# Second edge stage of a graph network kernel: own rows weighted on ScalarE, a quad ahead, in four copies instead of one VectorE operation

## The reference

```python
def gcn_conv(x, W, b, src, dst, n_nodes):
    xw = x @ W
    deg = segment_sum(ones, dst, n_nodes)
    dis = where(deg > 0, rsqrt(maximum(deg, 1e-12)), 0.0)
    norm = dis[src] * dis[dst]
    msgs = norm[:, None] * xw[src]
    return segment_sum(msgs, dst, n_nodes) + b
...
h = maximum(_layernorm(x), 0.0)
x = x + gcn(h)              # src, dst with a self-loop for every node
h = maximum(_layernorm(x), 0.0)
```

## Time and profile before

| | |
|---|---|
| time, median of 3 runs | 6671.95 us (6667.89 to 6674.51) |
| profiled execution: its own time | 6683.69 us |
| its span, first to last instruction | 6681.9 us |
| granted TensorE clock, mean | 0.848 of full |
| busy: PE, PEld | 4418.0 us (66%), 3717.4 us (56%) |
| busy: DVE, ACT, POOL | 3833.9 us (57%), 2944.6 us (44%), 3487.0 us (52%) |
| operation `OWN<-OWN,dis` on DVE, stages C1 and C2 | 98 times, median 693 ns |

### The profile page before, as it was taken

The page is one execution under the profiler, slowest core; times in us unless marked ns, Lnnn a source line. Parts: engine busy times, 40 slices in busy tenths (PEclk is TensorE's granted clock), DMA queues, the critical chain, the costliest instruction groups (busy, mean ns, idle before and its releaser), DMA issues. The chain is left out here.

```text
span 6681.9 us, 125449 instructions
## 1 busy us (share of the span) xinstructions
PE 4418.0 (66%) x28875; PEld 3717.4 (56%) x28950; DVE 3833.9 (57%) x13851; ACT 2944.6 (44%) x7261; POOL 3487.0 (52%) x4337
## 2 busy tenths in 40 slices
PE   4888888888788668877798966630660480282065
PEld 3666666666566666667787856630550370272065
DVE  5777777777544883347677767730650460261186
ACT  3777777777432333335576755530230130031043
POOL 3444444444470747327575665027457556556666
PEclk9999999999999659998999987765895795696576
DMA  3555555555442665448543444222232232232143
GB/s 98 184 187 187 187 187 186 186 186 186 128 115 70 198 181 136 115 122 218 151 118 96 113 113 116 82 69 53 73 95 53 61 103 58 51 102 70 43 115 91
DMA packets 1002707, 815.71 MB, mean 122 GB/s; under 512 B 103820, under 2 KB 836818, under 8 KB 1002616
## 3 DMA queue, kind: packets, MB, share of 16 engines
q1 hardware_dynamic: 908536, 650.27, 31.5%
q0 software_dynamic: 94080, 164.48, 10.3%
HBM read 359.28 MB, written 459.01 MB: 122 GB/s over the span
## 5 line engine op out<-in xcount | busy, mean ns | idle before, releaser
L839 POOL DMA_INDIRECT G<-table,idx_all x1568 | 1522.7, 971 | 1308.3 <-issue 670.6
L1411 PE MATMUL PS<-G,S 128*128 (+2 forms) x4312 | 852.3, 304 | 6.4 <-DMA G<-table,idx_all 2.4
L1411 PEld LDWEIGHTS PS<-G,S 128*128 128x128 f32 x4312 | 731.4, 220 | 55.8 <-issue 48.2
L839 POOL DMA_INDIRECT G<-table,idx_l x588 | 581.6, 989 | 336.2 <-issue 178.7
L1734 ACT ACTIVATE CR<-PS 65x128 f32<-65x128 f32 (+3 forms) x1078 | 289.1, 268 | 1021.2 <-PE PS L1411 1009.6
L1411 PE MATMUL PS<-CR,LO 97*128 97x128 f32 (+1 forms) x4312 | 655.3, 301 | 64.4 <-ACT CR L1734 64.4
L1408 PE MATMUL PS<-ident,ES 128*98 128x128 f32 x16 | 4.2, 420 | 1002.3 <-DVE ES L470 1002.3
L1411 PE MATMUL PS<-G,FS 128*65 (+2 forms) x3234 | 521.2, 301 | 216.9 <-DVE den L1343 100.7
L1411 PEld LDWEIGHTS PS<-CR,LO 97*128 97x128 f32 x4312 | 606.9, 217 | 75.7 <-ACT CR L1734 75.7
L792 POOL DMA_INDIRECT XIN<-in_x,idx_x x196 | 187.5, 957 | 846.0 <-ACT GN L1734 732.4
L470 DVE COPY ES<-G 128x392 f32<-128x392 f32 x4 | 2.1, 528 | 1016.5 <-DMA G<-table,idx_all 1016.5
(11 more groups left out here) (287 smaller groups left out, 11282.1 us busy)
## 6 DMA issues: line engine op xcount, KB each, us to landing
table<-G SPq DMA_DIRECT2D x392, 260.0 KB, 2.5
table<-G SPq DMA_DIRECT2D x392, 256.0 KB, 2.1
table<-RO SPq DMA_DIRECT2D x245, 256.0 KB
table<-RO SPq DMA_DIRECT2D x196, 260.0 KB
OWN<-table SPq DMA_DIRECT2D x196, 260.0 KB
XIN<-xrows SPq DMA_DIRECT2D x196, 256.0 KB
OWN<-table SPq DMA_DIRECT2D x147, 256.0 KB
xrows<-RB SPq DMA_DIRECT2D x147, 256.0 KB
```

The source lines that it names most:

```text
L839: g.indirect_dma_start(G[:, t, 0:w], None, TAB[s], bass.IndirectOffsetOnAxis(ap=idx[:, t:t + 1], axis=0)).then_inc(gat[t % 4].sem, 16)
L1411: return nc.tensor.matmul(o, l, r, start=start, stop=stop)
```

## The change

In C2 VectorE no longer multiplies OWN. ScalarE does it in four copies of 128 rows each, in place, with the row's weight as the factor of the copy; for quad n + 1 within its turn of quad n, and for quad 0 ahead of the loop. VectorE waits for a new semaphore, `oscale`, ahead of the combine. C1 keeps the operation on VectorE. SyncE's and TensorE's programs and all other stages stay as they are.

```diff
-            "C2": ("own", "bias", "comb", "x", "stats", "aggr", "rs", "nb"),
+            "C2": ("bias", "comb", "x", "stats", "aggr", "rs", "nb"),
...
+        oscale = steps("oscale", {"C2": ("own",)})
...
                 if kind in ("C1", "C2"):
-                    dve.wait_ge(own.sem, own.at(s, n, "rows"))
-                    ins = v.tensor_tensor(OWN[:, :, 0:D], OWN[:, :, 0:D], wide(dis2[:, ds(Q4, 4)], D), ALU.mult)
                     if kind == "C1":
+                        dve.wait_ge(own.sem, own.at(s, n, "rows"))
+                        ins = v.tensor_tensor(OWN[:, :, 0:D], OWN[:, :, 0:D], wide(dis2[:, ds(Q4, 4)], D), ALU.mult)
                         step(s, n, ins, "own")
                         dve.wait_ge(pd.sem, pd.last(s, n, "uT"))
                     else:
-                        ins.then_inc(vd.sem, 1)
                         dve.wait_ge(xin.sem, xin.at(s, n, "rows"))
                         step(s, n, v.tensor_tensor(XIN[:, :, :], XIN[:, :, :], on4(b2_r[:, :]), ALU.add), "bias")
+                        dve.wait_ge(oscale.sem, oscale.at(s, n, "own"))
                     aggregated(s, n)
...
+            def own_scaled(s, n):
+
+                Q4 = n * (-4) + 4 * LAST
+                act.wait_ge(own.sem, own.at(s, n, "rows"))
+                for j in range(4):
+                    i = f(OWN[:, j, 0:D], OWN[:, j, 0:D], ACT.Copy, scale=dis2[:, ds(Q4 + j, 1)])
+                i.then_inc(oscale.sem, 1)
...
                 if kind == "C2":
                     ahead(3, 2, 1)
                     sqrts(s, n)
+                    if not isinstance(n, int) or n < LAST:
+                        own_scaled(s, n + 1)
                     ahead(0)
                     act.wait_ge(st_t.sem, st_t.at(s, n))
                     scaled(s, n, ACT.Relu)
...
+                if kind == "C2":
+                    own_scaled(s, 0)
                 carried(s, 0, 0, 3, 2, 1, 0)
```

## The result

The changed kernel takes 6715.06 us (median of 4 runs, 6709.99 to 6717.87) beside 6670.3 for the kernel before: ratio 1.0066 (1.0048 to 1.0083), +45 us. The forecast was 6705, from 6684 to 6738.

The account below looks back on a forecast made before the run. In C2, XIN's load loop (6.81 us per turn) was taken as the bound; a new ring through OWN's load gives 32.6 turns at 7.66 and 14.4 at 7.18, +33 us: 6672 + 33 = 6705, range 6684 to 6738.

Parts of the forecast that it names:

- XIN's loop: C2: bias, combine and addition free XIN (3.23 us), its next load takes 3.58; 6.81 us per turn, the bound before.
- the removed 0.69: C2, VectorE: the own-rows multiplication, 0.69 us per quad, lies inside XIN's flight; removing it lengthens waits in turns already waiting.
- up to 19 us: C2, rival "faster", 5%: ring slack and VectorE's own chain the bound in 28 turns; up to -19 us, 6653.
- The rule of the most-contended engine: C2: relieve the busiest engine first, here VectorE; the whole 34 us would come off, 6638; weighed and rejected.
- Four copies cost 1.27: C2, ScalarE: own-row copies per quad, 0.39 us for the first and 0.295 for each of three more, 1.27 together.
- The ring: C2: own copies, CR, GN, its store, OWN's load, next own copies; 7.66 us per turn until 2426.5, 7.18 after.
- The links without the flight: C2's ring: copies 1.27, CR 0.17, GN 1.65, store issue 0.02, OWN's load behind the store 0.97; together 4.08 us.
- The flight: C2: OWN's load from issue to use, taken as 3.58 us while gathers run and 3.1 after.
- L: C2: symbol for OWN's flight from issue to use; a ring turn is 4.08 + L.
- The upper bound: C2: OWN's flight 4.53 us while gathers run and 3.58 after; turns of 8.61 and 7.66, +67 us.
- The slack elsewhere: C2: nothing but the ring ends last in a 7.66 us turn; XIN's path to the combine level with CR's.
- three signs of being wrong: C2: combines staying 6.8 us apart, GN's store preceding OWN's load by over 1.2, or OWN used in under 2.7.

Follow-up runs that it names:

- The doubled dose: The changed kernel with four more 128x128 copies per quad on ScalarE, eight in all; ratio 1.0158 to the kernel before, C2 432.1 us.

## Why the prediction was right

**XIN's loop bounds C2 before, and the removed 0.69 is covered.** Shown by the run with two buffers: all of the change's work moved, C2 as before. The prediction left room for up to 19 us in the turns in which VectorE did not wait for XIN, and there it was too generous: after the gathers VectorE waits for XIN in 1 of 11 turns in the kernel before and in all 11 with two buffers, and a turn takes 6.4 us in both. The load came just in time there, and ended last as soon as VectorE was earlier.

The rule of the most-contended engine (the Trainium skill, "Perfetto Trace Analysis", section "Identifying the Most-Contended Engine"), by which 34 us would have come off, was wrong for this change by itself. With XIN's loop out of the way, relieving VectorE did pay (C2 from 332.1 to 286.7).

**Four copies cost 1.27.** Measured 1.28 (at 2301.31 in the turn above). The doubled dose confirms that they count in full, 56.7 against 55 us. The Trainium skill ("ScalarE: Activation LUTs", section "What ACT_TABLE_LOAD costs") gives 186 ns and 0.833 ns per column, 93 more for each factor or bias read per row, and an overlap of 93 between neighbours; the estimate by that is 1.26 us for the four, and the trace agrees.

**The ring.** All links are in the trace in the order foretold, and each part that was taken out took ScalarE's wait for OWN (73.8 us) with it: the store (0.7 us left), the copies' work (4.0 us left, ratio 0.9997), the single buffer together with the copies' place behind the root (none left, ratio 0.9995). Two attempts at removing it through SyncE's order failed to bring all of the time back, as they made a loop through GN's store in one case and a longer flight of XIN in the other; by these alone a cost of the copies as such was not excluded. The run with two buffers, with all of the copies' work on ScalarE, excludes it.

**The sizes.** The links without the flight measured 2305.56 - 2301.31 = 4.25, not 4.08. Most of it is CR, which starts 0.02 behind the copies rather than 0.10 ahead of their end; the rest is hundredths in the other links. That is 0.17 x 47 = 8 us. The flight: a combine of the kernel after stands at

```profile
2425.51 0.69 DVE L1296 TENSOR_TENSOR U<-PS,OWN 128x512 f32<-128x512 f32 x1 [0.27 <-DVE XIN L1286]
```

so 31 turns took 8.13 us each and 17 took 7.26, and L was 8.13 - 4.25 = 3.88 while gathers ran, against 3.58 taken, and 3.01 against 3.1. (Read from issue to use, turn by turn, the means are 3.96 and 3.05.) This term, 0.3 x 31 = 9 us, was set by XIN's flight in place of OWN's own in such a burst. Together, less 1.5 us for the turns after the gathers, they are the 16 us by which C2 (+49.4) passes the forecast (+33). The forecast for C2 was thus a third too low. That the median, 6715, still came within 10 us of 6705 owes a few us to chance, since the medians differ by 45 us and C2 by 49. The upper bound had taken 4.53 from stage S2; single turns here reach that (up to 4.95, 4.43 in the turn above), the mean does not.

**The slack elsewhere.** VectorE's wait of over 1 us in each turn is there (3.12 in the one above), but ahead of the bias on XIN, not of the combine, since XIN's load goes out later too; the combines are 8.1 apart in the mean with gathers, just outside the 7.2 to 8.0 foretold. None of the three signs of being wrong came: combines 6.8 apart, the store over 1.2 us ahead of OWN (0.98 in the mean, 1.00 at most), OWN in use in under 2.7 us (2.88 at least). As foretold nothing but the ring set the turn: ScalarE waits for OWN in each one, and XIN, which the prediction had level with CR, came last ahead of the combine in 15 of 37, without holding up the ring. TensorE's granted clock was 0.66 of full in these 250 us, where the kernel before had 0.61, both between its levels of 1.2 and 2.4 GHz; ScalarE waited for TensorE once between 2180 and 2480, 0.9 us.

## What to carry to other kernels

An operation that moves to an engine with idle time takes a place in that engine's queue, and everything behind it inherits its wait. Before such a move write down the ring: what stands behind the moved work, which DMA is issued from that, and whether the moved work waits for a DMA queued behind it; here a single buffer and the order of the transfers on SyncE closed the ring. A busy share of 83% is no proof that an engine is the bound. VectorE waited for one load in 26 of 44 turns here, and removing work from it gained nothing, in the other turns either, until that load's loop was out of the way. After that the move paid 0.95 us per turn, and only with the copies at a place in ScalarE's queue where no chain ran through them.

## What the runs showed of the hardware

The place of a 256 KB transfer among its neighbours moved another's time from issue to use by some 0.6 us. XIN, issued 1.36 us behind OWN, took 3.68 us in the mean with gathers running; with a store issued between the two, 0.65 us ahead of XIN, it took 4.30, and after the gathers 3.26 and 3.86. Loads of OWN issued 0.98 behind a store and 0.59 ahead of XIN took 3.96 in the mean with gathers running and 3.05 without, as much as with no store ahead (3.04); so without gathers the store ahead of OWN costs it nothing. With XIN cut to a quarter the loads of OWN took 3.66 and 3.06, and C2 was 6.6 us shorter. Without the store ahead and with XIN 1.35 behind it, OWN was in use after 3.24 with gathers running. How the rest divides between the store and XIN's distance is open.
